# Post-norm transformer, two layers with experts: last stage split into attention of all batches and expert units of rows sorted by expert set

## The reference

```python
x = L0_attn_x                                   # 8 x 1024 x 256
x = layernorm(x + linear_attention(x))          # layer 0: 32 heads of 8, relu
x = layernorm(x + capacity_experts(x))          # 7 real experts of 1024 rows, top 2 of 8
x = layernorm(x + softmax_attention(x))         # layer 1: one head of 256, 1024 keys per batch
x = layernorm(x + grouped_experts(x))           # layer 1, below
# grouped_experts, xf = x as 8192 rows:
scores = sigmoid(xf @ gate.T)                   # 8 experts in 2 groups of 4
sfc = scores + corr_bias
# the group with the larger sum of its two best keeps its sfc, the other group's become 0
sel = top_k(sfc, 2)[1]; w = scores[sel] / (sum + 1e-20)
lat = xf @ fc1_w.T                              # 128 wide
comb = sum over e in sel of w_e * relu(lat @ w1[e].T)**2 @ w2[e].T
out = comb @ fc2_w.T + relu(xf @ up_w.T)**2 @ down_w.T   # shared part, 1024 wide
```

## Time and profile before

| What | Value |
|---|---|
| median of 3 runs | 1944.69 us (1942.36 to 1946.76) |
| profiled execution, its own time | 1951.98 us |
| its span, first to last instruction | 1950.2 us |
| PE matmul busy | 1814.9 us (93%), 11342 instructions |
| DVE busy | 1357.2 us (70%), 3290 |
| ScalarE busy | 856.5 us (44%), 1595 |
| POOL busy | 864.2 us (44%), 1167 |
| mean granted clock of PE | 0.979 of full speed |
| DMA | 132.49 MB, mean 68 GB/s |

### The profile page before, as it was taken

One profiled execution on the slowest core, in us unless ns is written; L12 is line 12 of the kernel. 1 busy time (PEld: TensorE's weight loads), 2 busy tenths in 40 slices (PEclk: granted clock), 3 DMA queues, 4 the chain that ended last, 5 costly groups with the idle time before them and its releaser, 6 DMA issues.

```text
span 1950.2 us, 34718 instructions
## 1 busy us (share of the span) xinstructions
PE 1814.9 (93%) x11342; PEld 1600.0 (82%) x11342; DVE 1357.2 (70%) x3290; ACT 856.5 (44%) x1595; POOL 864.2 (44%) x1167
## 2 busy tenths in 40 slices
PE   7999996699999989899999999999999989989996
PEld 6888885499999978788788888878878878878885
DVE  4688887544444556886886886886886786786674
ACT  4445543433333514445445445445455445445443
POOL 4267788521111232454454354364265255255054
PEclk9999997799999989999999999999999999999998
DMA  3211312332222431112211111121112113111011
GB/s 125 82 65 65 116 58 88 114 103 87 86 86 86 133 76 47 64 44 64 68 45 52 52 72 44 45 87 45 44 54 78 43 46 88 37 51 55 12 45 65
DMA packets 82053, 132.49 MB, mean 68 GB/s; under 512 B 11360, under 2 KB 62688, under 8 KB 81920
## 3 DMA queue, kind: packets, MB, share of 16 engines
q1 hardware_dynamic: 72400, 104.44, 15.9%
q0 software_dynamic: 9520, 26.36, 5.7%
HBM read 105.05 MB, written 25.72 MB: 67 GB/s over the span
## 4 chain that ended last, share of the span: by engine, by line
PE 57%; DVE 10%; issue 7%; ACT 3%; POOL 3%; DMA 1%; DVEq 0%; POOLq 0%; ACTq 0%
PE c_ps L118 9%; PE c_ps L119 9%; PE c_ps L120 9%; PE b_ps L118 5%; PE b_ps L120 5%; PE b_ps L119 5%; PE c_ps L133 2%; PE c_ps L135 2%; PE c_ps L134 2%; PE c_ps L2126 2%; DVE c_tmp L97 2%; PE c_ps L2174 2%; PE c_ps L2173 2%; PE c_ps L2172 2%; POOL c_pool_tmp L97 1%
## 5 line engine op out<-in xcount | busy, mean ns | idle before, releaser
L1625 POOL TENSOR_TENSOR c_place<-c_shared_place,c_place 128x512 fp32r<-128x512 f32 x256 | 324.0, 1295 | 190.9 <-ACT c_place L1804 120.2
L1616 POOL DMA_INDIRECT c_gathered<-expert_results,c_slots x112 | 112.4, 1003 | 323.8 <-DVE c_pre L1860 300.2
L2030 DVE SCALAR_TENSOR_TENSOR c_shared_place<-c_ps,c_shared_place 128x512 f32<-128x512 f32 x256 | 169.7, 683 | 47.3 <-ACT c_shared_place L1796 47.2
L118 PE MATMUL c_ps<-c_place 128*128 128x264 f32 (+1 forms) x520 | 150.6, 290 | 16.0 <-DVE c_place L1943 11.6
L1804 ACT ACTIVATE c_place<-c_shared_place 128x512 fp32r<-128x512 f32 x128 | 80.3, 630 | 178.3 <-DVE c_shared_place L2030 176.5
L133 PE MATMUL c_ps<-c_downT_hi,c_place 128*128 128x256 f32 x512 | 146.7, 286 | 8.5 <-POOL c_place L1625 8.5
L119 PE MATMUL c_ps<-c_place 128*128 128x264 f32 (+1 forms) x520 | 148.2, 285 | 0.0
L120 PE MATMUL c_ps<-c_place 128*128 128x264 f32 (+1 forms) x520 | 147.8, 284 | 0.0
L1102 POOL DMA_INDIRECT b_xs<-x_rows,expert_tokens x56 | 58.0, 1035 | 200.8 <-PE b_ps L1290 180.8
L134 PE MATMUL c_ps<-c_downT_lo,c_place 128*128 128x256 f32 x512 | 145.1, 283 | 0.0
L135 PE MATMUL c_ps<-c_downT_hi,c_place 128*128 128x256 f32 x512 | 145.1, 283 | 0.0
(11 more groups left out here) (444 smaller groups left out, 5964.3 us busy)
## 6 DMA issues: line engine op xcount, KB each, us to landing
c_x2T<-score_rows SPq DMA_DIRECT2D x64, 512.0 KB, 5.3
b_win_raw<-xT SPq DMA_DIRECT2D x8, 1024.0 KB, 6.4
a_x_rows<-x SPq DMA_DIRECT2D x8, 1024.0 KB, 5.4
x_rows<-a_x SPq DMA_DIRECT2D x8, 1024.0 KB, 4.5
c_pre<-x_rows SPq DMA_DIRECT2D x8, 1024.0 KB, 5.5
out<-b_win_raw SPq DMA_DIRECT2D x16, 512.0 KB
b_win_raw<-w_in SPq DMA_DIRECT2D x7, 1024.0 KB, 5.5
b_wout_raw<-w_out SPq DMA_DIRECT2D x7, 1024.0 KB, 6.2
```

The lines of the kernel that those rows point to most:

```text
L118: pe.matmul(out, lh, rh, start=(j == 0), stop=False)
L1616: pool.indirect_dma_start(rows[:, a, :], None, d["ys"], bass.IndirectOffsetOnAxis(ap=slots[:, a, t:t + 1], axis=0), bounds_check=TRASH + P ...
L1625: pool.tensor_tensor(hid_lo[:, place, :], square[:, place % RING, :], f32(hid_hi[:, place, :]), ALU.subtract).then_inc(hid_split, 1)
L2030: v.scalar_tensor_tensor(square[:, place % RING, :], ps[:, s_bank(unit, k - lag), :], 0.0, factor, ALU.max, ALU.mult).then_inc(s_free, 1)
```

## The change

stage_c is unrolled and runs in two parts. The engines' orders are no longer one list but three (PE, ScalarE, DVE), written out by functions; semaphore counts and PSUM banks are derived from them.

Part one: attention of all batches. PE works two tiles ahead of the mix (prob and the turned probabilities have two buffers). x2 of batch b+1 is finished in b: POOL gathers into a ring of four tiles, the first four of a batch already at the end of the batch before; ScalarE scales the two gathered rows ("weigh"), POOL adds them. Norm, logits and routing of batch b-1 are done in b for all 8 tiles at once. POOL then marks the rows (weights of the set, set flag) and counts rows of the lower set; PE sums the counts over partitions ("pos"), DVE adds them to positions, and POOL scatters each row, 270 values wide with its weights and token number, to `sorted` in DRAM: the lower set from the front, the upper from the end. Row buffers rotate over four batches.

Part two: 16 units of 512 rows. Unit 0 is the first half of the last batch, unsorted, with 8 experts; 14 sorted blocks have one set, 5 experts; the last unit is the block where the sets meet, with 8. The last half batch is routed and scattered inside unit 0. Each unit loads its block and a copy of its set's w1 and w2 (stored to DRAM once, at the start) into two alternating places; the row number of the set and block comes from a table that SP reads. Results are stored by POOL with indirect transfers to the token's own row.

```diff
+ROW = C + EXPERTS + GSIZE + 2
...
-    ORDER = [("q", 0), ("q", 1), ("q", 2), ("q", 3), ("keep", 0), ("v", 0), ("v", 1), ("keep", 1),
...
+    GATHER, RELU_RING, RING, BUFFERS = 4, 2, 4, 4
...
+    POSTS = [(b, 0, TILES) for b in range(LAST)] + [(LAST, 0, HTILES), (LAST, HTILES, TILES)]
+    EARLY_POST, LATE_POST = LAST, LAST + 1
...
+    def both(u):
+        return u in (0, UNITS - 1)
+    def picks(u):
+        return EXPERTS if both(u) else PICKS
+    def pick(u, k):
+        first_round = u + 1 if u else 0
+        return (first_round + k // GSIZE, k % GSIZE) if both(u) else (first_round, k)
...
+    def experts_of(u):
+        units, quarter = [], 0
+        for k in range(picks(u)):
+            units.append(("w1", u, k))
+            for _ in range(1 if both(u) or k < 3 else k - 1):
+                units.append(("down", u, quarter))
+                quarter += 1
+            if u == 0 and k == PICKS - 1:
+                units.append(("pos", LATE_POST))
+            if both(u) and k == PICKS + 1:
+                units.append(("comb_a", u))
+            if 0 < u < UNITS - 1 and k in (3, 4):
+                units.append((("x3T", "scoreT")[k - 3], u + 1))
+        assert quarter == QUARTERS
+        units.append(("comb", u))
+        if u == 0:
+            units += [("x3T", 1), ("scoreT", 1)]
+        return units
...
+    def tensor_order():
...
+        for b in range(BATCHES):
+            n = b + 1
+            for j in range(TILES - 3):
+                units += [("score", b, j + 2), ("turn", b, j + 1), ("mix", b, j)]
+                if j == (1 if b == LAST else 2) and b > 1:
+                    units.append(("pos", b - 2))
+            if b < LAST:
+                units += [("score", b, 7), ("turn", b, 6), ("x2T", n, 0), ("mix", b, 5), ("x2T", n, 1), ("q", n, 0), ("q", n, 1),
+                          ("turn", b, 7), ("mix", b, 6), ("score", n, 0), ("q", n, 2), ("q", n, 3),
+                          ("mix", b, 7), ("v", n, 0), ("score", n, 1), ("v", n, 1), ("v", n, 2), ("v", n, 3), ("turn", n, 0)]
+            else:
+                units += [("score", b, 7), ("turn", b, 6), ("mix", b, 5), ("turn", b, 7), ("mix", b, 6), ("pos", b - 1), ("x3T", 0), ("mix", b, 7)]
+        for u in range(UNITS):
+            ups = [("up", u, k) for k in range(UPS)]
+            units += ups[0:2] + ([("out", u - 1)] if u else []) + ups[2:4] + ([] if u else [("scoreT", 0)]) + [("latent", u)] + ups[4:UPS] + experts_of(u)
+        return units + [("out", UNITS - 1)]
...
+    def scalar_order():
...
+            weigh = [("weigh", n, t) for t in range(TILES)] if b < LAST else [None] * TILES
+            norm3 = [[("norm3", p, h)] if b else [] for h in range(2)]
+            units += [("turn", b, 1), ("exp", b, 2)] + weigh[1:3] + ([("odds", p)] if b else [])
+            units += [("turn", b, 2), ("exp", b, 3)] + weigh[3:5]
+            units += [("turn", b, 3), ("exp", b, 4)] + weigh[5:8]
+            units += [("turn", b, 4), ("exp", b, 5)] + norm3[0]
+            if b < LAST:
+                units += [("turn", b, 5), ("exp", b, 6), ("norm_x2", n, 0), ("turn", b, 6), ("exp", b, 7), ("norm_x2", n, 1), ("x2T", n, 0), ("x2T", n, 1), ("q", n, 0), ("q", n, 1)] + \
+                         norm3[1] + [("turn", b, 7), ("q", n, 2), ("q", n, 3)] + keep + beginning(n)
...
+    def vector_order():
...
+            route = [[(kind, p)] if b else [] for kind in ("logits", "route_a", "route_b", "route_c")]
+            ready = [("pos", b - 2)] if b > 1 else []
+            if b < LAST:
+                before = [[], [], [], stats[5:7], []]
+                between = [route[0], stats[0:2], ready + stats[2:5], stats[7:8] + [("ln2", n)], []]
+            else:
+                before = [[], route[1], route[2], route[3], []]
+                between = [route[0], ready, [], [], []]
+            for j in range(TILES - 3):
+                units += before[j] + [("max", b, j + 2), ("shift", b, j + 2), ("turn", b, j + 1), ("mix", b, j)] + between[j]
+            if b < LAST:
+                units += [("max", b, 7), ("shift", b, 7), ("turn", b, 6), ("x2T", n, 0), ("mix", b, 5), ("x2T", n, 1), ("q", n, 0), ("q", n, 1)] + route[1] + \
+                         [("turn", b, 7), ("mix", b, 6)] + route[2] + ([("factor", n + 1)] if n < LAST else []) + \
+                         [("max", n, 0), ("q", n, 2), ("q", n, 3), ("mix", b, 7)] + route[3] + beginning(n)
...
+                units += [("score_et", 0)] + ups[0:1] + [("ln3", LATE_POST)] + ups[1:3] + [("scoreT", 0), ("logits", LATE_POST)] + ups[3:4] + [("latent", 0)] + ups[4:5] + \
+                         [("route_a", LATE_POST)] + ups[5:6] + [("route_b", LATE_POST)] + ups[6:7] + [("route_c", LATE_POST)] + ups[7:UPS]
+            else:
+                units += ups[0:3] + [("out", u - 1, 0), ("out", u - 1, 1)] + ups[3:4] + [("stats4", u - 1, 0), ("stats4", u - 1, 1)] + ups[4:5] + [("latent", u)] + \
+                         [("stats4", u - 1, 2), ("stats4", u - 1, 3)] + ups[5:6] + ([("score_et", u + 1)] if u < UNITS - 1 else []) + ups[6:UPS] + [("ln4", u - 1)]
+            for k in range(picks(u) + 1):
+                units += ([("scale", u, k)] if k < picks(u) else []) + ([("product", u, k - 1)] if k else [])
+                if u == 0 and k == PICKS + 1:
+                    units.append(("pos", LATE_POST))
+                if 0 < u < UNITS - 1 and k in (4, 5):
+                    units.append((("x3T", "scoreT")[k - 4], u + 1))
...
+            def load_round(r, row):
+                user = 0 if r < 4 else r - 3
+                last = GSIZE * (r - 2 + 1) - 1 if r < 4 else PICKS - 1
+                sp.wait_ge(h_full, inner(user, UPS + last) + 1)
+                load_copies(r, (0, 1), row, w1_in)
+                sp.wait_ge(v_full, FULL[("comb", user), 0])
+                load_copies(r, (2, 3), row, w2_in)
...
+            def spread_scores(u):
+                sp.wait_ge(v_free, FREE[("scoreT", u), 0])
+                sp.dma_start(d["score_rows"][u:u + 1, 0:picks(u) * HALF].rearrange("a (r s) -> (a r) s", s=P), scoreT[0:picks(u) * HTILES, :]).then_inc(scores_stored, 16)
+                sp.wait_ge(scores_stored, 16 * (u + 1))
...
+            for u in range(1, UNITS - 1):
+                if u + 2 < UNITS:
+                    load_block(u + 2)
+                spread_scores(u + 1)
+                if u + 2 < UNITS - 1:
+                    load_round(u + 3, group_row(u + 2))
+                else:
+                    load_round(u + 3, P * (u + 3 - UNITS))
...
+            def add_results(b, t):
+                n, rows, two = TILES * (b - 1) + t, x_of(b)[:, t, 0:C], gathered[t % GATHER]
+                pool.wait_ge(weighed, n + 1)
+                pool.tensor_tensor(two[:, 0, :], two[:, 0, :], two[:, 1, :], ALU.add).then_inc(combine_chain, 1)
+                pool.wait_ge(combine_chain, n + 1)
+                pool.tensor_tensor(rows, rows, two[:, 0, :], ALU.add).then_inc(combined, 1)
...
+            for b in range(BATCHES):
+                if b:
+                    add_bias(b)
+                    scale_rows(b - 1)
+                if b > 1:
+                    mark_rows(b - 2)
+                if b < LAST:
+                    for t in range(TILES):
+                        add_results(b + 1, t)
+                        if t + GATHER < TILES:
+                            gather(b + 1, t + GATHER)
+                if b > 1:
+                    scatter(b - 2)
+                if b < LAST - 1:
+                    for t in range(GATHER):
+                        gather(b + 2, t)
+            scale_rows(EARLY_POST)
+            mark_rows(LAST - 1)
+            scatter(LAST - 1)
+            for u in range(UNITS):
+                for k in range(UPS + picks(u)):
+                    split(u, k)
+                    if u == 0 and k == UPS - 1:
+                        mark_rows(LATE_POST)
+                    if u == 0 and k == UPS + PICKS - 1:
+                        scatter(LATE_POST)
+                if u:
+                    store(u - 1)
+            store(UNITS - 1)
...
+                elif kind == "pos":
+                    p = unit[1]
+                    n = tiles_of(p)[2]
+                    c = p if p < LAST else LAST
+                    bank = bank_of((unit, 0))
+                    v.wait_ge(v_full, FULL[unit, 0])
+                    if p == LATE_POST:
+                        chain = Chain(v, logit_chain, len(POSTS) * LOGIT_STEPS)
+                        chain.step(v.tensor_scalar(tile_end[:], tile_row[:], float(HALF), None, ALU.add))
+                        chain.then(v.tensor_scalar, later[:], tile_end[:], bank[:, n:n + 1], None, ALU.is_gt)
+                        chain.then(v.scalar_tensor_tensor, table[:, 0:SINGLE], later[:], float(HALF), tile_row[:], ALU.mult, ALU.add)
+                        chain.step(v.tensor_scalar(table[:, SINGLE:2 * SINGLE], later[:], float(P), None, ALU.mult))
```

(9 more changed lines are left out.)

1411 lines of the change are left out of this document (782 added, 629 removed).

## The result

The changed kernel takes **1877.81 us** (median of 4 runs, 1877.18 to 1878.03) against 1945.22 for the kernel before (4 runs): ratio 0.9655, 95% interval 0.9638 to 0.9671, 67.4 us less. The forecast was 1861 with 1823 to 1924. Two executions that lie far from all others (9787.72 us in experiment 2, 4477.8 us of the kernel before beside the last three runs) are left out of the ratios, and nothing here explains them.

The account below looks back on a forecast made before the run. TensorE (PE) was taken to set the pace. Start 737.2, eight attention batches to 1283.6, unit 0 to 1340.9, fourteen units to 1814.1, unit 15 to 1852.1, end 14.5: span 1866.6, execution 1868.4, forecast 1861 us, range 1823 to 1924.

Parts of the forecast that it names:

- Fewer experts, 59.2 us: 14 of 16 units take 5 experts instead of 8: 42 products of 6 matmuls less on PE, 59.2 us.
- Attention alone, 68.5: Part one: a batch takes 68.5 us, from 66.0 of PE work and 2.5 of waits; ends 66.2 and 76.
- 2.5 us of waits: Seam of two batches: PE waits about 0.9 at x2T, 1.2 at q and 0.3 at the next first turning.
- small steps of POOL hold little, and bias ends before routing starts: Attention part: argument against DVE and POOL setting the pace; the 68.5 us takes nothing for holds.
- the start at 737.2: First batch: its start, counted back by the period from batch 3's start at 1188.2 us.
- the rival: Attention part: DVE and POOL set the pace, one hold per POOL add, mark and bias; period 76, total 1921; chance 0.19.
- Units, 33.8: Part two, five-expert units: 33.8 us each, from 33.1 of PE work and 0.7 of waiting.
- the 0.7 us of waits: Shared units: PE waits 0.7 us a unit instead of 4, since the order gives it cover; ends 0 and 4.
- Seam, 57.3 for unit 0: Between the parts: unit 0 takes 37.3 plus 20 us for DVE, marks, transfers and clock; ends 8 and 60.
- the hole I put at the second x3T: Seam: positions, scatters, landing, register load, block load and x3T take 22 us against 12 of PE work; 10 lost.
- The end, 14.5: From PE's last matmul: adds 2.7, chain 2.8, norms 2.3, four indirect stores 5.2, landing 1.5; ends 11 and 18.
- The one on the other side (units waiting for scores): Units' first scale: score copies landing 7 us later than counted decide, each us beyond costs 15; chance 0.07.

Follow-up runs that it names:

- experiment 2: Changed kernel with the bias added by POOL in 8 instructions of 128x256 where it was one of 128x2048; ratio 0.9649 to the kernel before.
- experiment 1: Kernel before, own order, experts 5 to 7 of every half cut to 4 columns and left out of the second product; 1896.19 us, ratio 0.9748.
- experiment 3: Changed kernel with the next batch's bias moved on POOL ahead of the last two of four tiles gathered in advance; 1868.45 us, ratio 0.9610.

## Why the prediction was right, and where it was not

The stretch from the first x2T to the end was 16.1 us longer than the sum. By its steps:

- *Fewer experts, 59.2 us.* Right: experiment 1 gives the full time of every matmul, and the counts are the predicted ones.
- *Attention alone, 68.5.* The period is right (68.52, 68.56), the tenth by luck: 2.5 us of waits were put down and 1.5 came (0.9 at x2T for ScalarE's norm, 0.4 for its second half, 0.2), while PE was busy for 66.9 us where the sum had 66.0. The step that failed is "small steps of POOL hold little, and bias ends before routing starts", with which I put the holds aside. The second half of that sentence is true only where POOL's queue is short. I had counted 31 us of indirect issues on POOL and never asked where in the batch they leave the bias. From batch 2 on the hold costs 2.3 us a period, 9.2 in four, 9.4 by experiment 3's median.
- *The ends of the attention part.* From the first x2T to unit 0's x3T it is 566.7 us and the sum had 557.2, 9.5 too little, which looks like the holds alone and is not. The last batch took 74.4 and not 66.9, the first 70.7 and not 68.5, and one period has 1.1 us that nothing explains, 10.8 together. Against them stand 10.8 us that the sum had before the first batch without meaning to: it placed the start at 737.2 by the period, where the first x2T of before is at 726.4. These two cancel by luck.
- The Trainium skill, "SBUF — State Buffer", section "Who interferes with whom", has the two engines exclude each other for whole instructions where DVE reads two SBUF inputs or works SBUF to SBUF in its faster modes. The trace agrees for the kinds it names: tensor_tensor held (0.69 to 1.23 us for 0.19 to 0.22), the one-input addition held for 3.68 us, the reciprocal not (0.55 beside POOL and alone). What I did with it was wrong in both directions: the rival put a price on every add and mark (76 a batch; adds and marks cost nothing that PE saw), the sum put none on the one instruction that met a chain.
- *Units, 33.8.* 33.4, fuller than forecast: the 0.7 us of waits were not there. That is 5 us over 13 units on the good side.
- *Seam, 57.3 for unit 0.* 54.97. The terms were as described (DVE's chains among the squares cost 4.8 us in PE's waits), but the hole I put at the second x3T was elsewhere: 4.1 us before the second product, for a split behind the four scatters, and 0.9 for the block. From the last scatter's end to the load of the block it took 2.5 us, where the sum had 4 for the landing and 1 for SP's register load; that last term no run shows by itself. The steps behind it, unit 1 and the last one, were 7.4 us longer than the sum. In them lie the clock after the seam (1.5 by experiment 3), DVE's score copy (1.6), and the waits for splits and comb in the last unit (2.6); the rest is not accounted for.
- *The end, 14.5.* 21.1 from PE's last end. The mis-sized term is the landing of the last stores: 1.5 taken, 8.3 measured after the last issue. The earlier trace rows had the end of before with 7.4 us from SP's issue to the end; I read it and did not use it.
- *Chips.* The sum took its start and its stage from a trace that is most likely of the second kind, and came back to the other by the 0.37% between the profiled execution and the median, 7 us, which is about what that trace had lost before the stage.
- *Rivals.* The one on the other side (units waiting for scores) was given 7 us of cover and has some 15. None of the rivals, nor the forecast, had a chip on which the gain is zero.

Net: +9.5 attention (9.2 of holds, 10.8 at the ends, -10.8 of start, 0.3 of rounding), -2.3 seam, +2.3 for the rest of the units, +6.6 end, 16.1.

## What to carry to other kernels

When work moves to an engine's queue, write down at what time of the period each long instruction on it will now start, and look which small chain of the neighbour engine falls under it; shift it in time, since here cutting it did not help the chain. Read the end of the kernel from its last issue to the end of the span and carry that number over whole. And run a large reordering on more than one chip before believing its gain: what was packed closer may cost on one what it gives on another.
